# A fused attention and ternary feed-forward block: the loop over head groups written out with three event tables, and work moved between engines at both ends

## The reference, cut to what matters

```
y = x * rsqrt(mean(x*x) + 1e-6) * rms_w           # RMS norm
q, k, v = y @ w_in.T                              # 32 q heads, 8 k heads, 8 v heads
q, k = rope(q), rope(k)                           # x1*cos - x2*sin, x2*cos + x1*sin
a = softmax(causal(q @ k.T / 8)) @ v
x = layernorm(x + (x + a @ w_out.T))
tern(t, th, sc) = sc where t > th, -sc where t < -th, else 0
x = layernorm(x + tern(x, .33, .5) @ (tern(w, .2, .6) + rram).T)
```

## Time and profile before

| | us |
|---|---|
| median of 3 runs (lowest, highest) | 1520.88 (1519.64, 1521.97) |
| profiled execution | 1519.98 |
| its span, first to last instruction | 1518.2 |

### The profile page before, as it was taken

How to read it: one execution, slowest core, us unless ns; L and a number is a source line. 1 busy time by engine, 2 the same in 40 slices (tenths; PEclk the granted TensorE clock), 3 DMA queues, 4 the chain that set the end, 5 groups by cost and what they waited for, 6 DMA issues and landing times.

```text
span 1518.2 us, 30199 instructions
## 1 busy us (share of the span) xinstructions
PE 1392.5 (92%) x7472; PEld 1145.0 (75%) x7472; DVE 1113.8 (73%) x2534; ACT 1080.9 (71%) x2277; POOL 837.5 (55%) x831
## 2 busy tenths in 40 slices
PE   3489999999989998999989998999989999996785
PEld 2368887888878887888878887888878888875664
DVE  2268777877777776877777776777777778787896
ACT  3277878777777787787767787787867778784442
POOL 1365666375646666475646665475636665561243
PEclk9699999999999999999999999999999999998998
DMA  5001211021101111121101101121101101111111
GB/s 180 14 26 30 70 32 29 26 55 43 35 20 51 46 33 30 27 54 47 29 24 50 48 27 31 29 50 50 27 22 50 51 24 29 31 48 35 35 50 55
DMA packets 50534, 62.30 MB, mean 41 GB/s; under 512 B 10672, under 2 KB 31408, under 8 KB 50352
## 3 DMA queue, kind: packets, MB, share of 16 engines
q1 hardware_dynamic: 50352, 60.20, 13.8%
HBM read 34.74 MB, written 4.46 MB: 26 GB/s over the span
## 4 chain that ended last, share of the span: by engine, by line
PE 78%; issue 7%; DVE 6%; POOL 3%; ACT 2%; DMA 2%; SPq 0%; DVEq 0%; ACTq 0%; POOLq 0%
PE s L1082 18%; PE x L1106 16%; PE t L1146 15%; PE x L1130 11%; PE ot L1048 8%; PE ot L1046 8%; DMA swapped<-flat 2%; PE x L1114 1%; DVE stats L833 1%; DVE prob_lo L993 1%; PE x L1033 1%; DVE prob L912 1%; POOL flat L667 1%; POOL flat L664 1%; PE x L1088 1%
## 5 line engine op out<-in xcount | busy, mean ns | idle before, releaser
L912 DVE CUSTOM_DVE_ANT_0 prob<-s,mask 128x896 f32<-128x896 f32 (+7 forms) x512 | 382.8, 754 | 170.6 <-PE s L1082 149.9
L739 ACT ACTIVATE prob_hi<-t 128x512 fp32r<-128x512 f32 x576 | 341.3, 592 | 173.9 <-PE t L1146 143.0
L993 DVE TENSOR_TENSOR prob_lo<-t,prob_hi 128x512 fp32r<-128x512 f32 x576 | 394.0, 686 | 75.5 <-ACT prob_hi L739 69.7
L1082 PE MATMUL s<-k_t,q_t 128*128 128x512 f32 (+3 forms) x1536 | 385.0, 370 | 31.3 <-POOL q_t L680 17.7
L766 ACT ACTIVATE prob<-prob,neg_max 128x896 f32<-128x896 f32 (+7 forms) x512 | 393.4, 770 | 22.6 <-DVE neg_max L912 18.5
L1146 PE MATMUL t<-ident,prob 128*128 128x128 f32 x2304 | 350.0, 275 | 18.4 <-issue 18.4
L1146 PEld LDWEIGHTS t<-ident,prob 128*128 128x128 f32 x2304 | 289.3, 141 | 96.5 <-issue 22.2
L1082 PEld LDWEIGHTS s<-k_t,q_t 128*128 128x128 f32 x1536 | 266.0, 196 | 89.4 <-DVE neg_max L912 32.2
L1046 PE MATMUL ot<-prob_hi,v_sb 128*128 128x512 f32 x576 | 246.4, 428 | 0.0
L1048 PE MATMUL ot<-prob_lo,v_sb 128*128 128x512 f32 x576 | 231.2, 401 | 1.0 <-DVE prob_lo L993 0.9
L706 POOL TENSOR_TENSOR o_lo<-o_raw,o_hi 128x256 fp32r<-128x256 f32 x128 | 94.3, 737 | 214.2 <-ACT o_hi L819 211.4
(11 more groups left out here) (93 smaller groups left out, 1958.5 us busy)
## 6 DMA issues: line engine op xcount, KB each, us to landing
swapped<-flat SPq DMA_DIRECT2D x320, 64.0 KB, 2.0
spread<-recip_rows SPq DMA_DIRECT2D x128, 128.0 KB
recip_rows<-turned SPq DMA_DIRECT2D x512, 0.5 KB
acc<-L_attn_x SPq DMA_DIRECT2D x4, 1024.0 KB, 8.5
raw<-L_attn_w_in SPq DMA_DIRECT2D x8, 512.0 KB, 5.5
raw<-L_attn_w_out SPq DMA_DIRECT2D x8, 512.0 KB, 4.6
out<-acc SPq DMA_DIRECT2D x16, 256.0 KB, 2.0
raw<-L_attn_w_in SPq DMA_DIRECT2D x16, 128.0 KB, 6.0
```

The source lines that it names most:

```text
L739: act.activation(prob_hi[:, u % 2, :], t_ps[u % 2][:, :], ACT.Copy).then_inc(prob_hi_done, 1)
L912: dve.tensor_tensor_reduce(out=prob_row(s, h), in0=s_ps[:, off:off + cols], in1=mask[:, KEYS - cols:KEYS], scale=-DH ** -0.5, scalar=3e38, ...
L993: dve.tensor_tensor(prob_lo[:, u % 2, :], t_ps[u % 2][:, :], prob_hi[:, u % 2, :].bitcast(F32), ALU.subtract).then_inc(prob_lo_done, 1)
L1082: mm = pe.matmul(s_ps[:, off + c * P:off + c * P + cols], q_t[:, h, s * P:(s + 1) * P], k_t[:, part, keys:keys + cols], start=(part == 0), ...
```

## The change

The hardware loop is gone: `first`, `opening`, six `middle` plans and `final` are written out one after the other. Waits compare with constants, and the `sem_inc` behind them (`met`) is gone everywhere. Where an engine has already waited for a semaphore's value in an earlier pass, it doesn't wait again. Three tables (OPENING, MIDDLE, FINAL) take the place of one, all with other places, and the order of `first` is a written list. The first four tiles of x are loaded by one DMA each. In `first` the rope (`ro`) and the low parts (`hl`) are on DVE and no longer on POOL. In `final` the ternary of the weight is an event of its own, `fl`, on POOL: its load on SP waits for the ternary before it (`ffn_w_done`) and no longer for the quarter's last part (`ffn_lo_done`); `fw` keeps transposes and parts. The ternary of the 14 row tiles (`x1`) goes to POOL, in three operations where DVE had two. The two last tiles stay on DVE.

```diff
-PROJECT = (
-    (((58, 76, 99, 119), (118, 137, 151, 181), (141, 157, 165, 181)), 100),
...
-FFN_IN = (331, 349, 400, 415)
-EARLY = (
-    (388, 415, 437, 437, 441, 460), (394, 435, 438, 460, 462, 467), (403, 440, 454, 462, 466, 491),
...
-    (588, 604, 615, 624, 637, 642), (600, 612, 625, 637, 639, 647)
+FIRST = (
+    ('xn', 0), ('xn', 1), ('xn', 2), ('sq', 0), ('norm', 0), ('norm', 1), ('xn', 3), ('norm', 2), ('w', 0),
+    ('w', 1), ('w', 2), ('w', 3), ('norm', 3), ('sq', 1), ('xn', 4), ('pj', 2, 0, 2), ('norm', 4), ('xn', 5),
+    ('sw', 2, 0, 2), ('ro', 2, 0, 2), ('pj', 2, 0, 0), ('vt', 2, 0), ('hl', 2, 0, 2), ('sw', 2, 0, 0),
+    ('consts',), ('ro', 2, 0, 0), ('pj', 2, 0, 1), ('sw', 2, 0, 1), ('xn', 6), ('norm', 5), ('hl', 2, 0, 0),
+    ('ex', 2, 0, 0), ('sc', 2, 0, 0), ('ro', 2, 0, 1), ('sc', 2, 0, 1), ('norm', 6), ('hl', 2, 0, 1), ('xn', 7),
...
+MIDDLE = dict(
+    SCORES=(
+        ((0, 4, 4, 9), (3, 9, 11, 12), 40, 93), ((11, 18, 21, 25), (24, 29, 29, 36), 63, 93),
...
+FINAL = dict(
...
+    FFN_IN=(
+        (299, 343), (353, 361), (369, 394), (401, 412)
+    ),
+    EARLY=(
+        (358, 414, 436, 442, 449, 459), (403, 423, 442, 456, 464, 485), (408, 445, 456, 470, 473, 493),
...
+        (582, 592, 613, 616, 626, 643), (590, 611, 619, 628, 635, 647)
...
-            one(-1, first)
-            met_counts.clear()
-            one(0, opening)
-            met_counts.clear()
-            with eng.Fori(1, LAST) as g:
-                one(g, body)
-            met_counts.clear()
-            one(LAST, final)
+            for g, plan in enumerate(plans, -1):
+                one(g, plan)
...
-            load_x(0)
+            for t in range(4):
+                sp.dma_start(acc[:, t, :], x_v[:, t, :]).then_inc(x_tile_in[t], 16)
...
-                        elif e[0] == "fw":
+                        elif e[0] == "fl":
 
                             n = e[1]
                             sp.wait_ge(wout_done, 2 * NG)
                             if n:
-                                sp.wait_ge(ffn_lo_done, n)
+                                sp.wait_ge(ffn_w_done, n)
...
+                        if e[0] == "fl":
+
+                            n = e[1]
+                            pool.wait_ge(ffn_in[0], 16 * (n + 1))
+                            pool.wait_ge(ffn_in[1], 16 * (n + 1))
+                            if n:
+                                pool.wait_ge(ffn_lo_done, n)
+                            pool.tensor_scalar(raw[:, 2, :], raw[:, 0, :], TH_W, SC_W, ALU.is_gt, ALU.mult
+                                               ).then_inc(tern_step, 1)
+                            pool.tensor_scalar(raw[:, 0, :], raw[:, 0, :], -TH_W, SC_W, ALU.is_lt, ALU.mult
+                                               ).then_inc(tern_step, 1)
...
+                            pool.tensor_tensor(raw[:, 2, :], raw[:, 2, :], raw[:, 0, :], ALU.subtract
...
+                            pool.tensor_tensor(raw[:, 2, :], raw[:, 2, :], raw[:, 1, :], ALU.add).then_inc(ffn_w_done, 1)
+                        elif e[0] == "x1":
+
+                            t = e[1]
+                            if t == 0:
+                                pool.wait_ge(ffn_lo_done, KC)
+                            else:
+                                pool.wait_ge(xq_done, t)
+                            pool.wait_ge(x1_done, t + 1)
+                            pool.tensor_scalar(tern_tile(t), acc[:, t, :], TH_X, None, ALU.is_gt).then_inc(below_done, 1)
+                            pool.tensor_scalar(below_tile(t), acc[:, t, :], -TH_X, None, ALU.is_lt).then_inc(below_done, 1)
+                            pool.wait_ge(below_done, 2 * t + 2)
+                            pool.tensor_tensor(tern_tile(t), tern_tile(t), below_tile(t), ALU.subtract
+                                               ).then_inc(tern_done, 1)
...
                         elif e[0] == "x1":
-                            if e[1] == 0:
-                                dve.wait_ge(ffn_lo_done, KC)
                             first_norm(e[1])
-                            below(e[1])
-                            ternary(e[1])
...
+                        elif e[0] == "ro" and plan is first:
...
+                            dve.tensor_tensor(turned_x, turned_x, sin_sb[rows, q_half(half)], ALU.mult
+                                              ).then_inc(products_done, 1)
+                            dve.tensor_tensor(x, x, cos_sb[rows, q_half(half)], ALU.mult).then_inc(products_done, 1)
...
+                            dve.tensor_tensor(x, x, turned_x, ALU.add).then_inc(roped, 1)
```

More of the change, by code:

```diff
@@ L64, in __init__, with number @@
         self.behind = [[] for _ in range(slots)]
-    def number(self, pads=0):
-        self.pads = pads
-        self.x = {("pad", n): n for n in range(pads)}
+    def number(self):
+        self.x = {}
         for u in range(len(self.ahead)):
@@ L136, in put @@
         placed.append((at, len(placed), e))
-    for b, s in [(0, s) for s in range(2, NT)] + [(1, s) for s in range(NT)] + [(2, 0), (2, 1)]:
-        if last and b == 2:
-            continue
-        scores, exps, norm, spread = SCORES[b * NT + s - 2]
+    for b, s in [(0, s) for s in range(2, NT)] + [(1, s) for s in range(NT)] + (
+            [] if last else [(2, 0), (2, 1)]):
+        scores, exps, norm, spread = at_pass["SCORES"][b * NT + s - 2]
         for h in range(HG):
@@ L147, in body_plan @@
         put(spread, ("rs", b, s))
-    for n, (chunks, turn) in enumerate((FIRST_HALF,) + PROJECT):
+    for n, (chunks, turn) in enumerate(at_pass["PROJECT"], 0 if opening else 1):
         b, half = divmod(n + 1, 2)
-        if n == 0 and not opening or b == 2 and last:
-            continue
         for c, places in zip((2, 0, 1), chunks):
@@ L232, in seq_block @@
     first, opening = first_plan(), body_plan(True, False)
-    body, final = body_plan(False, False), body_plan(False, True)
-    first.base = 0, 0
-    opening.number((len(body.x) - len(opening.x)) % RING)
-    opening.base = first.uses, len(first.x) - opening.pads
-    body.base = final.base = (opening.base[0] + opening.uses - body.uses,
-                              opening.base[1] + len(opening.x) - len(body.x))
-    opening.past, body.past, final.past = first, body, body
-    assert list(body.x)[-2 * RING:] == list(opening.x)[-2 * RING:]
+    middle, final = [body_plan(False, False) for _ in range(1, LAST)], body_plan(False, True)
+    plans = [first, opening] + middle + [final]
+    first.base, first.past = 0, None
+    for past, plan in zip(plans, plans[1:]):
+        plan.base, plan.past = past.base + len(past.x), past
     x_v = x.rearrange("b (t p) d -> p (b t) d", p=P)
@@ L311, in seq_block @@
         x_in = [sem(f"x_in{n}") for n in range(4)]
+        x_tile_in = [sem(f"x_tile_in{n}") for n in range(4)]
         ffn_in = [sem(f"ffn_in{n}") for n in range(2)]
@@ L410, in wait_x_free @@
             n, past, back = plan.x[e] - RING, plan, 0
-            if n < plan.pads:
+            if n < 0:
                 if plan is first:
                     return
-                n = n if n < 0 else n - RING
                 past, back = plan.past, 2
-                n += past.uses
-                while n >= len(past.x):
-                    n -= RING
             kind, *what = list(past.x)[n]
-            assert len(what) >= 2 or not back or kind == "norm"
             if kind == "pj":
@@ L431, in wait_x_free @@
             elif kind == "w":
-                wait(eng, win_done, g, 4, 4 + what[0] + 1)
+                wait(eng, win_done, g, 4, 4 + what[0] + 1 - 2 * back)
             elif kind == "wo":
-                wait(eng, wout_done, g, 2, what[0] + 1)
+                wait(eng, wout_done, g, 2, what[0] + 1 - back)
             elif kind == "fw":
@@ L657, in one @@
                             x, turned_x = flat[rows, n % 2, :], swapped[rows, n % 2, :]
[L658 removed]
+                            if plan is opening and half:
                                 pool.wait_ge(table_in[half], 32)
+                                pool.wait_ge(parts_done, 3)
                             wait(pool, swapped_in[n % 2], g, swaps(10), swaps(n))
[L661 removed]
                             pool.tensor_tensor(turned_x, turned_x, sin_sb[rows, q_half(half)], ALU.mult
@@ L1150, in one @@
                     events(plan.behind[u])
-                    if 0 < u <= plan.units or u == 0 and plan in (body, final):
+                    if 0 < u <= plan.units or u == 0 and plan not in (first, opening):
                         values(u - 1)
```

200 lines of the change are left out of this document (94 added, 106 removed), and 82 rows, old and new, of tables (EARLY, FIRST, OUTPUT, PROJECT).

## The result

The kernel after takes 1474.2 us in the median of 4 runs (1473.25 to 1477.1); the kernel before took 1521.43 in 4 runs on the same chip (1519.64 to 1522.47). The ratio is 0.9694, with an interval of 0.9677 to 0.9711. The forecast was 1451 with a range of 1428 to 1476: faster, as forecast, but 23 us above the value, outside the forecast's own 1436 to 1464 and just inside the wider range. The profiled execution took 1474.06, its span 1472.2, against a sum of 1448.0.

The account below looks back on a forecast made before the run. PE was taken to bound the kernel, busy 1392.5 of 1518.2 us. 1518.2 - 22.9 - 9.0 - 20.3 - 4 - 14 = 1448.0, with 1.8 around the span and 0.9 for the median 1451; own range 1436 to 1464, 8 in 10 1428 to 1476.

Parts of the forecast that it names:

- The loop: Six middle passes, 1011.9 us before: gaps and low clock behind them go, -22.9, and MIDDLE's places bring -9.0.
- constants for register waits and the lost `sem_inc` I put at nothing: Middle passes: no gain, since they run in sequencers beside 164 us of PE work; at most 3.3 us a pass.
- MIDDLE's places: -1.5 a pass: Six middle passes: the new table brings -9.0 in all, bounds +6 to -29.
- second rival: Tables bring more: middle passes -3.3 in place of -1.5, opening -12 in place of -4; total 1432, chance 0.15.
- The start: Up to the first unit: from 71.8 to 51.5 us, -20.3, bounds -14 to -26.
- third rival: Start held by transfers (swaps, landing of x): only -12 comes, total 1459, chance 0.06.
- The opening: Opening pass, 187.3 us: norms of tiles 8 to 15 spread, projections and scores earlier; -4, bounds +4 to -12.
- The weight's ternary: Last pass: PE's waits for it fall from 18.2 us to 9, low clock shortens by 1; -10, bounds 0 to -19.
- the danger to `o_lo`: Last pass: `o_lo` for the output projections waits in POOL's queue behind a waiting `fl`; no size given.
- The row ternary: Last pass: POOL compares at 0.9 us, 4.6 us a tile, stretch from 85 to 81; -4, bounds +10 to -15.
- first rival: POOL bounds the end: compares cost 1.29, late stretch takes 95, weight gives 3 us less; total 1468, chance 0.17.
- fourth rival: Straight code stalls on instruction fetching, 56 more packets for six passes: 258 us on top, total 1709, chance 0.02.

Follow-up runs that it names:

- experiment 1: Kernel before with only the hardware loop written out as six equal passes, waits comparing with constants; table, `sem_inc` and engines as before: 1490.24 us, ratio 0.9795.
- experiment 2: As experiment 1, with the `sem_inc` behind the waits left out too; places and engines of the kernel before: 1482.93 us, ratio 0.9752.
- experiment 9: Kernel after with the middle passes' places set back to the one table of before: 1466.92 us, ratio 0.9642.
- experiment 5: Kernel after with the weight's ternary back on DVE at the place `fw`, the load still at the place `fl`: 1489.53 us, ratio 0.9806.
- experiment 11: Kernel after with before's places in middle and last passes, rows' ternary back on DVE, weight's ternary on POOL ahead of its transposes: 1466.05 us, ratio 0.964.
- experiment 3: Kernel after with the ternary of the 14 row tiles back on DVE, six steps ahead of the transposes: 1465.63 us, ratio 0.9652.
- experiment 10: Kernel after with POOL's two row-tile compares replaced by multiplications (one constant, then two), ternary not computed: 1464.89 us in one execution.
- experiment 4: Kernel after with the row ternary shared: one compare stays on POOL, the combined second operation goes to DVE: 1466.12 us, ratio 0.9636.
- experiment 12: As experiment 11, but rows' ternary shared: one compare on POOL, second operation on DVE six steps ahead of the transposes: 1475.69 us, ratio 0.9703.

## Why the prediction was right or wrong

**The loop: right in size, wrong in its parts.** -31.9 forecast, -30.3 measured, but by two errors that cancel. The gaps and the clock behind them were -22.9 and no gap is left: in the timeline after, the unit that opens the second middle pass follows the last matmul of the pass before,

```profile
400.41 0.44 PE L1088 MATMUL ot<-prob_lo,v_sb 128*128 128x512 f32 x1
400.70 0.60 PE L1186 MATMUL t<-ident,prob 128*128 128x128 f32 x4
...
564.58 0.60 PE L1186 MATMUL t<-ident,prob 128*128 128x128 f32 x4
```

The step "constants for register waits and the lost `sem_inc` I put at nothing" failed: together with the other engines' turns of the loop they bring 2.2 us a pass (experiments 1 and 2) of the 3.3 given as the most; how much of the first 1.7 is the register waits alone is open. The argument, that 164 us of PE work cover them and that the last pass is as full, overlooked that the last pass pays for `sem_inc` too: it wasn't a pass without that cost. The step "MIDDLE's places: -1.5 a pass" failed with the wrong sign: +1.1 (experiment 9). For six passes that is +6.7, just outside the bounds of +6 to -29. The second rival, that the tables bring more, is refuted for both tables.

**The start: right.** -22.5 against -20.3. First projection at 20.27 (forecast 20.1), first scores 39.06 (38.8), second scores 44.98 (44.5), first unit 49.25 (51.5). The step by which it is better is the last one: 4.3 us from the second scores to the first unit where before took 6.8. The third rival is out: x landed earlier, and a swap was waited for by only 1.2 us. Of the gain 7.4 is the engine of rope and low parts, about 1.3 the tiles of x; the rest, about 14, is the order of `first`, by subtraction and not by a run.

**The opening: wrong by 4.7.** -4 forecast, +0.7 measured. OPENING brings nothing in time: with the old table it takes 188.1 (experiment 2). In other traces of the same opening it takes 187.6 to 191.6, never the 183.3 of the forecast. Its idle time of PE is 9.9 against 10.4. What the prediction aimed at did shrink: PE's waits for the scaled tiles of x (us, times, longest), first before (window 66 to 112), then after (49 to 92),

```profile
PE x L1066 <- DVE raw L891: 6.5, 4, 2.1
```

```profile
PE x L1106 <- DVE raw L943: 4.4, 2, 2.6
```

are 2.1 us less, but others came in: 1.8 for ACT's `flat`, 1.2 for `prob`. And PE was busy 1.2 us longer (178.13 against 176.90). What is left of the waits is in part the scalings themselves, slow in both kernels beside POOL's rope. All eight before (min, median, max in ns), then the first slow one after and POOL at that time:

```profile
L891 DVE TENSOR_SCALAR raw<-acc,rstd x8: 476/538/1474, 79.4 to 137.6; 128x512 f32<-128x512 f32 x8
```

```profile
61.33 1.37 DVE L943 TENSOR_SCALAR raw<-acc,rstd 128x512 f32<-128x512 f32 x1
```

```profile
61.15 1.26 POOL L693 TENSOR_TENSOR swapped<-swapped,sin_sb 64x512 f32<-64x512 f32 x1 [1.43 <-DMA swapped<-flat]
62.38 1.46 POOL L695 TENSOR_TENSOR flat<-flat,cos_sb 64x512 f32<-64x512 f32 x1
```

The same scaling takes 0.48 alone; this one began 0.2 us behind a two-input operation of POOL and ended 0.3 us behind its end. By the Trainium skill, "SBUF — State Buffer", section "Who interferes with whom", a DVE operation in a two-port mode and a GpSimd operation shut each other out, and the one issued first holds the ports until it is done; the rows agree. The step that failed is the -4 itself: of the 10.4 idle only the norms' waits were aimed at, and they gave 2.1. Why the pass got no shorter even by these isn't shown by any run.

**The weight's ternary: right in what it brought, by sizes that made up for each other.** PE's waits for it are 3.3 against 9, but the stretch takes 47 against 45 to 46: of the 14.9 us that went from these waits, PE's idle time in the stretch (20.2, now 11.8) gives back 8.4, since PE waits there for `prob_lo`, `neg_max` and `q_t` now. POOL's compare with a multiplication took 1.93, not 0.9. The bound "0 to -19" and the danger to `o_lo` were both real, as experiments 5 and 11 show: done at `fw` on DVE nothing of the gain is left, and at the old places on POOL 6 us of the last pass are given back.

**The row ternary: the step that failed.** "I take 0.9, between the two by its one input". Measured 1.50 and 1.53, above both ends: the bounds by the nearest rows, 0.5 and 1.29, did not hold it; having one input in place of two did not make it cheaper. In POOL's timeline one tile is

```profile
1372.56 1.51 POOL L668 TENSOR_SCALAR raw<-acc 128x512 f32<-128x512 f32 x1
1374.04 1.51 POOL L669 TENSOR_SCALAR raw<-acc 128x512 f32<-128x512 f32 x1
1375.63 1.31 POOL L671 TENSOR_TENSOR raw<-raw 128x512 f32<-128x512 f32 x1
1377.02 0.19 POOL L608 TENSOR_SCALAR inv_std<-moments 128x1 f32<-128x1 f32 x1
1377.30 0.56 POOL L611 TENSOR_TENSOR inv_std<-inv_std,neg_half 128x1 f32<-128x1 f32 x1
...
1379.21 1.50 POOL L668 TENSOR_SCALAR raw<-acc 128x512 f32<-128x512 f32 x1
```

6.65 us from tile to tile, where the sum had 4.6: 4.3 of ternary, then two inverse deviations, and hardly any idle time between them. PE's idle time before these transposes that ended with the ternary (us, times), before and after:

```profile
  DVE raw L856: 1.5, 3
```

```profile
  POOL raw L671: 19.7, 10
```

With 1.5 in place of 0.9 the prediction's own formula gives 14 x 4.6 + 32.6 = 97 for POOL, waits included; the stretch takes 99, with 86.7 of it busy. So the first rival's mechanism is there (its 95, at 1.29 a compare), only dearer, and its 1468 lies nearer to 1474 than the forecast. But the 14 us that the rival put to POOL are not confirmed: with the ternary off POOL the row tiles still take 91, not 81. By the Trainium skill, "GPSIMD Engine Reference", section "Elementwise — side-by-side cycle accounting", a short body (k ≤ 2) takes 1.03 cycles an element and two-input operations are priced apart; the prediction's estimate from it was 0.6 us: that is met by the form with two multiplications (0.62) and by none of the others, so here the measurement decides.

The sentence that POOL's new work would slow nothing on DVE isn't borne out either: the norm of a row tile, a `tensor_scalar` from SBUF to SBUF, stayed on DVE. Its mean is 620 ns after against 529 before, and 528 in experiment 3, 1 us over the stretch.

**What of the 20 us is explained.** Taking the ternary off POOL gives 8.0 back (experiment 3: 245.4 for the last pass against 253.3), a cheaper form 8.5 (244.8). The other 12 did not come back by relieving POOL: the forecast had added the weight's gain and DVE's relief, but experiment 3 with the first and experiment 10 with both have a last pass no shorter than experiment 2 at before's places with neither (245.4). The waits of experiment 3 show where they go: at the row tiles' new places PE waits for the ternary (13.9 us, before 1.5) and DVE for PE (10.4, before 2.5). Which places of the last table do it isn't isolated; experiment 11, meant to show it, brought a wait of its own, and another placing of `fl` was not run. That cause stays open.

**By its own signs.** The prediction called itself wrong if the last pass took over 247: it took 253.3, so by that sign the part on the last pass is wrong, although the total lies in the range. The other two signs held (middle passes below 166, first unit before 58). A one-input compare was to take 0.5 to 1.3 us and took 1.5; POOL was to be over 90% busy among the row tiles and was 88%, DVE near 75% and was 62%. That the total stays in its range, with 2 us to spare, is owed to the other parts, which came out within 5 us of their terms, and to errors in the loop that cancel.

**Found besides.** Experiments 3, 4, 9 and 11 take 1465.6 to 1466.9 and can't be told apart, each 7 to 9 us faster than the kernel after. Old middle places together with the split of experiment 4 were not run; if their gains of 6.7 and 8 us add up, they would give near 1459, and experiment 12 shows that such sums can fail.

## What to carry to other kernels

Before elementwise work goes to another engine, have a row of that engine for that very form, number of operations and constants included; where there is none, a duration between two other forms is no estimate and their ends are no bounds. When a loop is written out, the gap at the taken branch is only the visible part: what it charges inside the passes, with the bookkeeping that it needs, has to be measured on one written-out version; here it was 2.2 us of 165 a pass, not nothing. Work taken off a full engine shortens a stretch only if the order in the queues lets it: here PE and DVE waited for each other with neither full. A table of places that is worked out for the whole kernel is to be tried pass by pass: here the new one was a loss in the passes that make up two thirds of the time.

## What the runs showed of the hardware that was not expected

- A POOL `tensor_scalar` on 128x512 fp32 took 1.50 us with one operation (compare or multiplication), 1.93 with a compare and a multiplication, and 0.62 with two multiplications: of the forms seen, one with two operations was the fastest. The last figure and that of the single multiplication are from one execution.
- In experiments 1 and 2 written-out passes took 1.7 us less of 165 than the gap at the branch and the clock behind it account for, and leaving out the increment behind each wait gave 7 us over the kernel, though PE was 99% busy in these passes.
- Five more passes of straight code brought no stall: PE is busy 162.79 of 163.40 us in a middle pass. The instruction queue that the fourth rival reckoned with moved fewer packets than before, 60 against 74, where the rival had 56 more, and the page's other one 72 against 108:

```profile
q8 instruction: 60, 0.98, 0.3%
```
